# ScalarE's queue taken step by step, between engines that go two steps at a time, in a two-layer transformer kernel on one core

## The chip, the cores and the metric

The kernel runs on one core of a Trainium2 chip, as one launch. The metric is the device time in microseconds (us) of that launch; lower is better. TensorE (PE in the profile, its weight loads PEld), VectorE (DVE), ScalarE (ACT), GpSimd (POOL) and SyncE (SP, which here only issues DMAs) each run a queue of their own, written out by the kernel, and meet only at semaphores.

## The reference

Two layers over x of 32 batches x 256 tokens x 128 channels. Both have 16 heads of 8 channels and a mixture of 16 experts, of which each token takes two. Layer 0 has biases and a position term in its scores; layer 1 has an expert shared by all tokens in addition. Cut to what matters:

```python
h = _layernorm(x, axis=-1) * (1 + ca) + sa
x = x + ga * _L0_attn_ref(h, ...)      # scores = q k^T / sqrt(8) + slope * distance; softmax; probs v; Wo
h = _layernorm(x, axis=-1) * (1 + cb) + sb
x = x + gb * _L0_ffn_ref(h, ...)       # top 2 of 16 experts, gated, weighted sum
...                                    # modulation of layer 1
h = _layernorm(x, axis=-1) * (1 + ca) + sa
x = x + ga * _L1_attn_ref(h, ...)
h = _layernorm(x, axis=-1) * (1 + cb) + sb
x = x + gb * _L1_ffn_ref(h, ...)       # top 2 of 16 experts, and a shared expert
```

## The kernel before

**Units and steps.** A unit is one batch in one layer (64 units). Every engine walks over the same steps; a unit takes 16 of them until the next one follows, and each piece of a unit's work is tied to a step counted from the unit's start. Several units are therefore under way at once, at different stages. Steps run from -44 to beyond 1008.

**Scores and exponentials.** In each step TensorE makes, for one head of one unit, the scores with queries down (`ps_s`, L1230), of which VectorE takes the row maxima (`mx`, L1641), and, for one head of an earlier unit, the transposed scores with the maximum already subtracted (`ps_st`, L1236), of which ScalarE takes the exponential (`prob`, L877, 128x512). There are two banks of each. So the scores of step s wait until the maxima and the exponential of step s-2 are done (L1219 and L1224).

**Jobs.** All other matrix work of a step is in `jobs(step)`. It uses two PSUM banks, one for even and one for odd steps. By step modulo 16 (the constant `JOBS`):

- 0, 4, 8, 12: probabilities times values (`av`, L1099), copied out by ScalarE (`take_o`, L813) in the same step
- 1 and 11: the shared expert's first layer (L1195; layer 1 only), with a tanh on ScalarE (L866)
- 2 and 15: transposes of the attention result (L1107), read by VectorE
- 5: transposes of the normalised rows and of the context, each copied out by ScalarE (L805, L935)
- 6: transposes of the maxima and of the second normalised rows (L1157), each copied by ScalarE (L775, L943)
- 7: ranks of tokens among the experts, and the shared expert's second layer (L1203; layer 1 only), read by VectorE
- 9: projections of q and k (L1121), copied by ScalarE (L821/822 or L824/825)
- 10: output projection and router, read by VectorE; ScalarE makes the first bf16 part of q and k (L911), which needs nothing of this step
- 13: nothing on TensorE, a second bf16 part on ScalarE (L915)
- 14: transposes of the maxima and the values, each copied by ScalarE (L775, L927)
- 15 on ScalarE also: the normalisation (`xn`, L784)

**Experts.** Work on the experts comes in quads of four blocks with its own steps (transpose L1050, gate and up L1068, transpose L1080, down L1087), each followed by an activation on ScalarE (L834, L842 or L846, L853, L860). From about the sixteenth unit on three quads fall on every 32 steps, in even and odd steps, and in a job they come ahead of the unit's own work.

**Order of the queues.** TensorE's loop is by pairs: scores(s), scores(s+1), jobs(s), jobs(s+1). VectorE's is by pairs: maxima(s), maxima(s+1), rest(s), rest(s+1). ScalarE's is by pairs as well, with its exponentials in the place of the maxima; its `rest` holds all that is not an exponential. POOL's and SP's loops go by single steps. `free_bank` makes a job wait for the readers of the bank of two steps earlier. An engine's instructions go in the order of its queue, and a wait holds back all that is behind it.

Of the kernel before, what the change touches and what calls it, by code (L numbers as in the profile page):

```python
# [56 lines left out]
FIRST = -44  # L57
SETUP = -14
# [46 lines left out]
def at(step, after):  # L105

    n, k = divmod(step - after, H)
    return Unit(n) if k == 0 and 0 <= n < UNITS else None


def head_at(step, after):

    n, k = divmod(step - after, H)
    return (Unit(n), k) if 0 <= n < UNITS else (None, None)
# [20 lines left out]
STEPS = max(COMBINE) + 8  # L135
# [7 lines left out]
def quad_at(step, stage):  # L143

    for quick, after in enumerate(STAGE[stage]):
        q = Quad(QUAD[step - after]) if step - after in QUAD else None
        if q and q.quick == quick:
            return q
# [18 lines left out]
def build(nc, io, out):  # L167
    with ExitStack() as ctx:
# [215 lines left out]
        CLEAR = 6  # L384
# [366 lines left out]
        def _(sc):  # L751
# [6 lines left out]
            def setup():  # L758

                sc.wait_ge(rest_loaded, 16 * REST_LOADS)  # L760
                sc.activation(c_th[1][:], c_t[1][:], ACT.Tanh, scale=0.5).then_inc(c_tanh, 1)

            def clear_slots(i, part):

                if i == 0 and part == 0:
                    sc.wait_ge(dve_const, 6)
                n = NB // CLEAR
                sc.dma_start(slot_dram[i].rearrange("(j p) d -> p j d", p=P)[:, part * n:(part + 1) * n, :],
                             sh_out[:, 0:1, :].broadcast_to([P, n, D])).then_inc(slots_clear[i], 16)
# [39 lines left out]
            def take_o(u, g):  # L809
                sc.wait_ge(av_mm, u.count(4, g + 1))  # L810
                if g == 0 and u.has(2):
                    sc.wait_ge(ot_mm, u.count(2, -2))
                sc.activation(o_sb[u.par][:, g, :], ps_job[BANK[f"av{g}"]][:, 0:S], ACT.Copy).then_inc(o_ok, 1)  # L813
# [13 lines left out]
            def take_blocks(q):  # L827

                sc.wait_ge(blk_mm, q.no + 1)
                if q.no:  # L830
                    sc.wait_ge(gu_mm, q.before + 1)
                if q.tail and q.lane and q.nth == 0:
                    sc.wait_ge(av_mm, 4 * UNITS)
                sc.activation(h_blk_t[q.lane], ps_lane[q.bank][:], ACT.Copy).then_inc(blk_t_ok, 1)  # L834

            def tanh_gate(q):

                if q.no:
                    sc.wait_ge(*act_done(Quad(q.before)))
                if q.layer == 0:  # L840
                    sc.wait_ge(clip_ok, q.no * 2 + 1)
                    sc.activation(th_sb[0], g_sb[:].rearrange("p j f -> p (j f)"), ACT.Tanh, scale=0.5 * ALPHA).then_inc(th_ok, 1)  # L842
                else:
                    sc.wait_ge(gu_mm, q.no + 1)
                    gate = ps_lane[q.bank][:].rearrange("p (j g f) -> p j g f", j=QB, g=2)[:, :, 0, :]
                    sc.activation(th_sb[q.lane].rearrange("p (j f) -> p j f", j=QB), gate, ACT.Tanh, scale=0.5).then_inc(th_ok, 1)  # L846
# [8 lines left out]
            def take_y(q):  # L855

                sc.wait_ge(down_mm, q.no + 1)
                if q.no:
                    sc.wait_ge(*y_freed(q))
                sc.activation(y_sb[q.lane], ps_lane[q.bank][:], ACT.Copy).then_inc(y_ok, 1)  # L860
# [4 lines left out]
                    sc.wait_ge(sh_act_ok, u.count1(FC, c))  # L865
                sc.activation(sh_th[:], ps_job[BANK[f"sh{c}"]][:, 0:S], ACT.Tanh, scale=0.5).then_inc(sh_th_ok, 1)  # L866

            def exponentials(step):

                u, k = head_at(step, ST_AT)  # L870
                if u:
                    sc.wait_ge(st_mm, u.count(16, k + 1))
                    if k >= 8:
                        sc.wait_ge(av_mm, u.count(4, (k - 8) // 4 + 1))
                    elif u.has(1):
                        sc.wait_ge(av_mm, u.count(4, (k + 8) // 4 - 3))
                    sc.activation(prob[:, (k ^ 1) % 8, :], ps_st[k % 2][:], ACT.Exp).then_inc(exp_done, 1)  # L877

            def rest(step):

                for g in range(H // 4):
                    u = at(step, AT[f"av{g}"])
                    if u:
                        take_o(u, g)
                q = quad_at(step, "blocks")
                if q:
                    take_blocks(q)
                q = quad_at(step, "tanh")
                if q:
                    tanh_gate(q)  # L890
                q = quad_at(step, "act_t")
                if q:
                    take_act(q)
                q = quad_at(step, "down")
                if q:
                    take_y(q)
                u = at(step, -33)
                if u:
                    norm_apply(u)
                u = at(step, AT["h_t"])  # L900
                if u:
                    take_h(u)
                u = at(step, AT["qk"])
                if u:
                    take_qk(u)
                u = at(step, -22)
                if u:
                    sc.wait_ge(qk_ok, u.count(2, 2))
                    if u.has(1):
                        sc.wait_ge(parts_stored, u.count(96, 0))  # L910
                    sc.activation(qk_part[:, 0, :], qk_f[:], ACT.Copy).then_inc(qk_hi, 1)  # L911
                u = at(step, -19)
                if u:
                    sc.wait_ge(qk_r, u.count(1, 1))
                    sc.activation(qk_part[:, 1, :], qk_rest[:], ACT.Copy).then_inc(qk_mid, 1)  # L915
                for half in range(2):
                    u = at(step, AT[f"max_t{half}"])
                    if u:
                        take_max_t(u, half)
                u = at(step, AT["v"])  # L920
                if u:
                    sc.wait_ge(mxt0_v_mm, u.no + 1)
                    if u.has(2):
                        sc.wait_ge(av_mm, u.count(4, -4))
                    if u.no < 2:
                        sc.wait_ge(dve_const, 5)
                    sc.activation(v_ext[u.par][:, :, :, 0:DH],  # L927
                                  ps_job[BANK["v"]][:, S:2 * S].rearrange("p (t h d) -> p t h d", t=TT, h=H),
                                  ACT.Copy).then_inc(v_ok, 1)
                u = at(step, AT["ctx_t"])  # L930
                if u:
                    sc.wait_ge(h_ctx_mm, ctx_turn(u))
                    if u.has(1):
                        sc.wait_ge(wo_rt_mm, u.no)
                    sc.activation(ctx_t[:], ps_job[BANK["ctx_t"]][:, S:2 * S], ACT.Copy).then_inc(ctx_ok, 1)  # L935
                u = at(step, AT["h2_t"])
                if u:
                    sc.wait_ge(mxt1_h2_mm, h2_turn(u))
                    if u.has(1):
                        sc.wait_ge(wo_rt_mm, router_turn(u) - 1)  # L940
                    if u.no > B:
                        sc.wait_ge(sh_mm, u.count1(FC, 0))
                    sc.activation(h2_t[:], ps_job[BANK["h2_t"]][:, S:2 * S], ACT.Copy).then_inc(h2_ok, 1)  # L943
                for c in range(FC):
                    u = at(step, AT[f"sh{c}"])
                    if u and u.layer == 1:
                        tanh_shared(u, c)
                u = at(step, 77)
                if u:
                    sc.wait_ge(dz_ok, u.no + 1)  # L950
                    if u.layer == 1:
                        sc.wait_ge(z_ok, u.count1(1, 1))
                    if u.has(1):
                        sc.wait_ge(w_ok, u.count(2, 0))
                    if u.no > B:
                        sc.wait_ge(sg_ok, u.count1(1, 0))
                    n = 1 + u.layer
                    sc.activation(dz_th[:, 0:n, :], dz[:, 0:n, :], ACT.Tanh, scale=0.5).then_inc(top_tanh, 1)
                u = done_at(step, -2)
                if u:  # L960
                    first_rows(u)

            for step in range(FIRST, STEPS, 2):
                if step == SETUP:
                    setup()
                for s in (step, step + 1):
                    if s in range(40, 40 + 10 * 3 * CLEAR, 10):
                        clear_slots(*divmod((s - 40) // 10, CLEAR))
                exponentials(step)
                exponentials(step + 1)  # L970
                rest(step)
                rest(step + 1)


        @block.tensor
# [796 lines left out]
```

## Time and profile before

| | us |
|---|---|
| median of three runs | 1706.36 |
| lowest and highest of them | 1699.0, 1709.52 |
| the profiled execution | 1704.48 |
| its span, from first to last instruction | 1702.7 |

Busy shares of the span: TensorE 84%, VectorE 77%, ScalarE 68%, GpSimd 60%. Matmuls are pipelined and their ends are modelled, so TensorE's share is not a measure of its peak. The mean granted clock of TensorE was 0.948. The exponentials run from 75.9 us to 1528.4 us; behind that comes a tail of expert work. A row of the time-ordered view gives start and duration in us, then engine, line, operation, output and input, and in brackets the idle time in front of it and what ended it. Neighbouring equal instructions are merged into one row with their number (x2 for the two exponentials of a pair).

### The profile page before, as it was taken

The numbers are of one execution on the slowest core, as the hardware profiler recorded it, in microseconds if no ns is written. First come the engines' busy times: TensorE is split into PE (matmuls) and PEld (weight loads), VectorE is DVE, ScalarE is ACT, GpSimd is POOL, SyncE is SP. The second block draws the span as 40 slices with busy tenths as digits, with TensorE's granted clock in tenths as the row PEclk, the third lists the DMA queues.
The fourth block names the chain that finished last, engine by engine and source line by source line (L and its number), as shares of the span: only waits on it lengthen the run. The fifth ranks groups of instructions, "written<-read, shape, count | busy, mean of one in ns | idle before, by whom it ended". The sixth has DMA issues, their size and how long they took to land.

```text
span 1702.7 us, 44918 instructions
## 1 busy us (share of the span) xinstructions
PE 1425.2 (84%) x13909; PEld 920.9 (54%) x13909; DVE 1317.6 (77%) x3968; ACT 1163.5 (68%) x2708; POOL 1015.0 (60%) x1440
## 2 busy tenths in 40 slices
PE   2788887899899889988999989998999979886642
PEld 1244444465565556655666656665666646655542
DVE  5679898888888898889888898888888857643522
ACT  1488886788677777777777767777778757662422
POOL 1223336733675778577866778576756783577573
PEclk9999999999999999999999999999999989997966
DMA  6766666445555655566455656566556655344443
GB/s 202 174 149 158 154 153 147 127 118 124 137 144 129 141 126 148 139 143 141 122 146 139 133 125 153 132 142 137 136 142 157 145 127 126 102 118 128 138 129 86
DMA packets 392007, 234.70 MB, mean 138 GB/s; under 512 B 29007, under 2 KB 380561, under 8 KB 391267
## 3 DMA queue, kind: packets, MB, share of 16 engines
q1 hardware_dynamic: 356675, 188.82, 46.1%
q0 software_dynamic: 16384, 33.59, 7.4%
q10 hardware_dynamic: 18720, 9.44, 2.0%
q8 instruction: 121, 1.98, 0.5%
q14 instruction: 107, 0.88, 0.2%
HBM read 123.49 MB, written 108.17 MB: 136 GB/s over the span
## 4 chain that ended last, share of the span: by engine, by line
PE 36%; DVE 22%; POOL 22%; issue 13%; DMA 4%; ACT 1%; SPq 1%; POOLq 0%; DVEq 0%; ACTq 0%
DVE mx L1641 10%; POOL slot_dram L672 8%; PE ps_job L1099 7%; PE ps_s L1230 5%; POOL y_in L693 5%; PE ps_q L1068 4%; PE ps_q L1087 2%; PE ps_st L1236 2%; PE ps_q L1050 2%; PE ps_job L1120 2%; PE ps_q L1080 2%; POOL ln_rs L638 1%; PE ps_job L1195 1%; POOL qk_part L720 1%; PE ps_job L1203 1%
## 5 line engine op out<-in xcount | busy, mean ns | idle before, releaser
L1641 DVE TENSOR_REDUCE mx<-ps_s 128x2 f32<-128x512 f32 x1024 | 655.0, 681 | 107.8 <-PE ps_s L1230 105.9
L877 ACT ACTIVATE prob<-ps_st 128x512 f32<-128x512 f32 x1024 | 559.0, 595 | 80.7 <-PE ps_st L1236 80.1
L1230 PE MATMUL ps_s<-k_stk,q_stk 51*128 51x256 bf16 x2048 | 357.6, 282 | 89.9 <-DVE mx L1641 60.0
L1236 PE MATMUL ps_st<-q_stk,k_stk 53*128 53x256 bf16 x2048 | 350.9, 280 | 4.7 <-ACT prob L877 4.5
L1099 PE MATMUL ps_job<-prob,v_ext 128*32 128x256 f32 x4096 | 286.0, 398 | 24.8 <-issue 12.2
L672 POOL DMA_INDIRECT slot_dram<-h_row,slot x256 | 256.2, 1001 | 70.9 <-issue 64.2
L1230 PEld LDWEIGHTS ps_s<-k_stk,q_stk 51*128 51x128 bf16 x2048 | 142.5, 96 | 265.3 <-DVE mx L1641 163.4
L693 POOL DMA_INDIRECT y_in<-y_dram,slot x224 | 222.5, 993 | 84.8 <-issue 49.5
L1099 PEld LDWEIGHTS ps_job<-prob,v_ext 128*32 128x32 f32 x4096 | 115.9, 111 | 130.7 <-issue 31.3
L813 ACT ACTIVATE o_sb<-ps_job 128x256 f32<-128x256 f32 x256 | 96.8, 378 | 107.1 <-PE ps_job L1099 98.0
L716 POOL TENSOR_TENSOR qk_rest<-qk_f,qk_part 128x512 f32<-128x512 f32 x64 | 74.4, 1163 | 137.8 <-ACT qk_part L911 137.5
L1236 PEld LDWEIGHTS ps_st<-q_stk,k_stk 53*128 53x128 bf16 x2048 | 139.2, 96 | 16.5 <-ACT prob L877 6.3
L636 POOL TENSOR_SCALAR ln_ve<-ln_mv 128x2 f32<-128x2 f32 x128 | 28.8, 225 | 189.0 <-DVE ln_mv L1413 183.3
L1068 PE MATMUL ps_q<-wgu,h_blk_t 128*128 x704 | 116.3, 297 | 0.0
L1068 PEld LDWEIGHTS ps_q<-wgu,h_blk_t 128*128 128x128 f32 x704 | 98.6, 194 | 9.4 <-issue 7.7
L1087 PE MATMUL ps_q<-wd,act_t 128*128 x704 | 99.8, 285 | 3.1 <-ACT act_t L853 3.1
L720 POOL TENSOR_TENSOR qk_part<-qk_rest,qk_part 128x512 bf16<-128x512 f32 x64 | 74.3, 1160 | 41.7 <-ACT qk_part L915 41.1
L638 POOL TENSOR_TENSOR ln_rs<-ln_ve,neg_half 128x2 f32<-128x2 f32 x128 | 91.9, 718 | 10.7
L1087 PEld LDWEIGHTS ps_q<-wd,act_t 128*128 128x128 f32 x704 | 86.6, 194 | 19.7 <-issue 19.7
L1050 PE MATMUL ps_q<-ident,h_blk 128*128 128x128 f32 x376 | 65.8, 302 | 35.2 <-DMA h_blk<-slot_dram 30.3
L1107 PE MATMUL ps_job<-ident,o_sb 128*128 128x128 f32 x512 | 80.8, 282 | 1.2 <-DVE sh_act L1599 1.2
L711 POOL TENSOR_TENSOR act<-th_sb,u_sb 128x256 f32<-128x256 f32 x48 | 35.3, 734 | 68.3 <-DVE th_sb L1583 68.2
(211 smaller groups left out, 2885.8 us busy)
## 6 DMA issues: line engine op xcount, KB each, us to landing
part_dram<-qk_part SPq DMA_DIRECT2D x128, 192.0 KB
q_stk<-part_dram SPq DMA_DIRECT2D x128, 192.0 KB
k_stk<-part_dram SPq DMA_DIRECT2D x128, 192.0 KB
h_blk<-slot_dram SPq DMA_DIRECT2D x94, 256.0 KB, 3.2
y_dram<-y_sb SPq DMA_DIRECT2D x88, 256.0 KB, 2.4
part_dram<-qk_part SPq DMA_DIRECT2D x128, 128.0 KB
mod_in<-row_dram SPq DMA_DIRECT2D x64, 192.0 KB
slot_dram<-sh_out ACTq DMA_DIRECT2D x18, 512.0 KB, 4.6
```

The costliest lines, as they stand in the source:

```text
L638: pool.tensor_tensor(ln_rs[i][:], ln_ve[i][:], neg_half[:], ALU.pow).then_inc(ln_rstd[i], 1)
L672: pool.indirect_dma_start(slot_dram[u.group % 3], bass.IndirectOffsetOnAxis(ap=slot[u.group][:, i:i + 1], axis=0), h2_row[u.no % len(h2_ro ...
L693: pool.indirect_dma_start(y_rows[y_buf(u)[0]][:, j // 2, j % 2, :], None, y_dram[u.group % 3], bass.IndirectOffsetOnAxis(ap=slot[u.group][ ...
L813: sc.activation(o_sb[u.par][:, g, :], ps_job[BANK[f"av{g}"]][:, 0:S], ACT.Copy).then_inc(o_ok, 1)
L877: sc.activation(prob[:, (k ^ 1) % 8, :], ps_st[k % 2][:], ACT.Exp).then_inc(exp_done, 1)
L1050: mm = pe.transpose(ps_lane[q.bank][:, j * P:(j + 1) * P], h_blk[q.blk][:, j * D:(j + 1) * D], ident[:])
L1068: mm = pe.matmul(b[:, j * P:(j + 1) * P], h_blk_t[q.lane][:, j * P:(j + 1) * P], wgu[q.layer][:, w], start=q.layer == 1, stop=True)
L1087: mm = pe.matmul(ps_lane[q.bank][:, j * P:(j + 1) * P], act_t[q.lane][:, j * P:(j + 1) * P], wd[q.layer][:, bass.ds(expert[q.bank][j], P)] ...
L1099: mm = pe.matmul(columns(f"av{g}")[32 * i:32 * i + 32, 0:S], v_ext[u.par][:, kt, h, :], prob[:, h % 8, kt * S:(kt + 1) * S], start=kt == 0 ...
L1230: mm = pe.matmul(ps_s[j % 2][:, t * S:(t + 1) * S], q_stk[us.tri][r0:r0 + R_BIAS, hp, t * P:(t + 1) * P], k_stk[us.tri][r0:r0 + R_BIAS, hp ...
L1236: mm = pe.matmul(ps_st[k % 2][:, t * S:(t + 1) * S], k_stk[ut.tri][r1:r1 + R_MAX, hp, t * P:(t + 1) * P], q_stk[ut.tri][r1:r1 + R_MAX, hp, ...
L1641: dve.tensor_reduce(mx[:, hp // 4, :, 4 * par + hp % 4], ps_s[j % 2][:].rearrange("p (t s) -> p t s", s=S), AX_X, ALU.max).then_inc(max_do ...
```

## The change

ScalarE's loop becomes one over single steps: exponential of s, rest of s, exponential of s+1, rest of s+1. No instruction is added or removed, no semaphore value changes, and the loops of the other engines stay. What changes place, once per pair, is the exponential of the odd step s+1: it goes behind the rest of the even step s, with every wait in that rest. (The issue of a DMA that clears slots, which was ahead of a pair's exponentials, is now ahead of its own step's.)

```diff
-            def exponentials(step):
-
+            for step in range(FIRST, STEPS):
+                if step == SETUP:
+                    setup()
+                if step in range(40, 40 + 10 * 3 * CLEAR, 10):
+                    clear_slots(*divmod((step - 40) // 10, CLEAR))
                 u, k = head_at(step, ST_AT)
                 if u:
                     sc.wait_ge(st_mm, u.count(16, k + 1))
@@
                     sc.activation(prob[:, (k ^ 1) % 8, :], ps_st[k % 2][:], ACT.Exp).then_inc(exp_done, 1)
-
-            def rest(step):
-
                 for g in range(H // 4):
                     u = at(step, AT[f"av{g}"])
                     if u:
@@
-
-            for step in range(FIRST, STEPS, 2):
-                if step == SETUP:
-                    setup()
-                for s in (step, step + 1):
-                    if s in range(40, 40 + 10 * 3 * CLEAR, 10):
-                        clear_slots(*divmod((s - 40) // 10, CLEAR))
-                exponentials(step)
-                exponentials(step + 1)
-                rest(step)
-                rest(step + 1)
```

## Rows read from the trace of the kernel before

**Rows 1.** Stages of 50 us: busy us (instructions) by engine, clock, DMA share, GB/s
```profile
150.00:200.00 50.00, 43.13 (x493) 23.69 (x486) 45.03 (x141) 40.10 (x96) 15.82 (x33) 1.00 0.69 156
...
500.00:550.00 50.00, 46.67 (x486) 30.50 (x485) 41.59 (x123) 39.37 (x91) 26.17 (x41) 0.97 0.54 134
```

**Rows 2.** The same stages, exponentials (L877) alone: busy us (count), clock, DMA share
```profile
150.00:200.00 50.00, 25.04 (x47) 1.00 0.69 156
...
500.00:550.00 50.00, 19.78 (x36) 0.97 0.54 134
```

**Rows 3.** Waits of the whole span: us in total, times, longest
```profile
PEld ps_s L1230 <- DVE mx L1641: 163.4, 315, 4.0
...
DVE th_sb L1583 <- ACT th_sb L846: 33.6, 15, 3.8
...
PE ps_s L1230 <- ACT prob L877: 17.1, 33, 3.8
```

**Rows 4.** ScalarE in order of time, one unit without experts
```profile
161.17 1.08 ACT L877 ACTIVATE prob<-ps_st 128x512 f32<-128x512 f32 x2
162.12 0.65 ACT L911 ACTIVATE qk_part<-qk_f 128x512 bf16<-128x512 f32 x1
...
164.37 0.39 ACT L813 ACTIVATE o_sb<-ps_job 128x256 f32<-128x256 f32 x1 [0.63 <-PE ps_job L1099]
...
164.65 0.62 ACT L915 ACTIVATE qk_part<-qk_rest 128x512 bf16<-128x512 f32 x1
...
166.22 0.36 ACT L775 ACTIVATE mx_t<-ps_job 16x256 bf16<-16x256 bf16 x1
...
166.75 0.86 ACT L784 ACTIVATE xn<-x,ln_shift,ln_rs 128x128 f32<-128x128 f32 x2
```

**Rows 5.** TensorE in order of time, the same unit
```profile
160.34 0.28 PE L1230 MATMUL ps_s<-k_stk,q_stk 51*128 51x256 bf16 x1
...
162.40 0.27 PE L1230 MATMUL ps_s<-k_stk,q_stk 51*128 51x256 bf16 x1
...
163.25 1.07 PE L1099 MATMUL ps_job<-prob,v_ext 128*32 128x256 f32 x16 [0.45 <-issue]
164.25 0.28 PE L1230 MATMUL ps_s<-k_stk,q_stk 51*128 51x256 bf16 x1
...
164.48 0.27 PE L1230 MATMUL ps_s<-k_stk,q_stk 51*128 51x256 bf16 x1
...
165.57 0.60 PE L1107 MATMUL ps_job<-ident,o_sb 128*128 128x128 f32 x4
166.10 0.28 PE L1230 MATMUL ps_s<-k_stk,q_stk 51*128 51x256 bf16 x1
...
170.28 0.28 PE L1230 MATMUL ps_s<-k_stk,q_stk 51*128 51x256 bf16 x1 [0.58 <-DVE mx L1641]
...
177.52 0.28 PE L1230 MATMUL ps_s<-k_stk,q_stk 51*128 51x256 bf16 x1
```

**Rows 6.** GpSimd in order of time, one row of the same unit
```profile
162.85 1.16 POOL L716 TENSOR_TENSOR qk_rest<-qk_f,qk_part 128x512 f32<-128x512 f32 x1 [4.64 <-ACT qk_part L911]
```

**Rows 7.** ScalarE: first and last of 31 rows, a unit with experts, layer 0
```profile
502.81 1.08 ACT L877 ACTIVATE prob<-ps_st 128x512 f32<-128x512 f32 x2 [0.82 <-PE ps_st L1236]
...
522.92 1.10 ACT L877 ACTIVATE prob<-ps_st 128x512 f32<-128x512 f32 x2
```

**Rows 8.** ScalarE: first and last of 33 rows, a unit of layer 1
```profile
1060.41 1.08 ACT L877 ACTIVATE prob<-ps_st 128x512 f32<-128x512 f32 x2
...
1083.24 1.08 ACT L877 ACTIVATE prob<-ps_st 128x512 f32<-128x512 f32 x2
```

**Rows 9.** TensorE in order of time: two jobs of odd steps, a clock dip
```profile
805.21 1.93 PE L1099 MATMUL ps_job<-prob,v_ext 128*32 128x256 f32 x16 [0.59 <-issue]
...
1064.40 1.14 PE L1203 MATMUL ps_job<-wsd,sh_act 128*128 128x128 f32 x8
...
1079.57 1.13 PE L1195 MATMUL ps_job<-h_t,wsgu 128*128 128x256 f32 x4
```

## The prediction

> **What bounds the kernel now.** I read the stages of 50 us first, then the waits, then the order of time engine by engine. In a stage without experts (150 to 200 us) VectorE is busy 45.0 of 50 us, TensorE 43.1, ScalarE 40.1; from 500 to 550 us, with experts, TensorE 46.7, VectorE 41.6, ScalarE 39.4 [rows 1]. No engine is full. The exponentials give the pace: 47 in 50 us, or 1.06 us a step, in the first, 36 or 1.39 us in the second [rows 2]. The waits show a ring of TensorE and VectorE, alternately late: TensorE's score loads waited 163.4 us for maxima, and its score matmuls only 17.1 us, 33 times, for an exponential [rows 3]. So ScalarE is now hardly ever late at the scores. It has slack, and the question is how much of it the new order takes.
>
> The order of time shows why. The pair's exponentials follow the scores at once, and they fill the very time in which TensorE does the even step's job: the exponentials of steps 12 and 13 lie ahead of 163.6, and the values' matmul of step 12 runs from 163.25 to 164.25; ScalarE then sat idle 0.63 us and copied its result at 164.37 [rows 4, 5]. With the new order only one exponential fills that gap; the other has to come after the copy.
>
> **The change, part by part.** No instruction is added, and the work per pair is the same, so there is no cost in busy time. A pair starts with two steps of scores on TensorE; then come J(s) and J(s+1), the job times. The exponential of s+1 must be done before the scores of s+3, the second step of the next pair.
> - Before, it starts about half a microsecond behind that of s. Two take 1.08 us, and the next activation starts 0.95 us after the first [rows 4], so each occupies 0.48.
> - After, it starts 0.05 us (rounded from the gap seen at the value's copy) behind the end of J(s), plus R, the issue time of the even step's activations that wait for J(s).
> - From the start of an exponential to the scores that it releases are 0.75 us: the second of the pair at 161.17 starts at 161.65, and the scores of step 13 at 162.40 [rows 4, 5].
> - Left to itself TensorE would start the scores of s+3 at the end of J(s) plus J(s+1) plus 0.23 (164.25 to 164.48) [rows 5].
>
> The lateness is therefore 0.05 + R + 0.75 - 0.23 - J(s+1) = R + 0.57 - J(s+1). For the eight pairs of a unit without experts:
> - 12: R 0.28 (164.37 to 164.65), J(13) nothing: 0.85. The same at 0 in layer 0, where step 1 is empty.
> - 14: two copies, R 0.53 (166.22 to 166.75), J(15) 0.53 (165.57 to 166.10): 0.57 [rows 4, 5].
> - 4: R 0.28, J(5) four transposes like J(15), some 0.55: 0.30.
> - 6: R as at 14; J(7) a few 16-column matmuls, an estimate of 0.25: 0.85.
> - 10: no wait for the job, but the q and k part goes ahead of the second exponential, 0.52 us from 162.12 on [rows 4]; that exponential was already the last thing awaited at 162.40, so 0.52.
> - 8: J(9), two projections, is longer than R + 0.57: nothing. 2: nothing on ScalarE in its rest: nothing.
>
> The sum is 3.9 us in a unit of 17.18 us (160.34 to 177.52) [rows 5]. It isn't all paid, since TensorE also waits for maxima: at 170.28 it sat 0.58 us for them [rows 5]. I carried the new order by hand through this unit, each start the latest of its own queue, its operand and its bank, with VectorE's queue in the same manner. The stalls at steps 15, 1 and 3 add up to about 1.65; VectorE's maxima take back 0.9 to 1.0 at steps 4 and 5; steps 7 and 9 add 0.3 and 0.4. Step 13 adds another 0.25, because the job behind it waits for VectorE until 163.25 anyway. The end is later by 1.3 to 1.55: say 1.45.
>
> With experts, a quad in an odd job lengthens J(s+1) and hides the late exponential; one in an even job adds half a microsecond to R. The same walk through the layer-0 unit that starts at 502.81 (20.11 us) [rows 7] ends 1.0 to 1.1 later. Nothing is lost at step 15 (a quad in step 13); the rest comes at steps 1, 7, 9, 11 and 13. In layer 1 the shared expert puts about 1.1 us each into steps 7, 11 and 1 [rows 9], which clears the lateness at 0 and 6; but the copies and quads of even steps, up to three activations ahead of an exponential, put it back: the walk through the 22.83 us from 1060.41 [rows 8] ends 1.4 later.
>
> Sum: the first 14.5 units run before the experts start, 14.5 x 1.45 = 21; 17.5 units of layer 0 with experts x 1.1 = 19; 32 of layer 1 x 1.4 = 45; together 85 us. Nine units end a group, where VectorE plans for about 3 us and everything else waits for it; I take those as absorbing all of theirs, 9 x 1.3 = 12. That leaves 73. Before the first exponential and after the last nothing changes, since a rest follows a rest as before. 1704.5 + 73 = 1777.5 for the profiled execution, which lies 1.9 under the median; I forecast 1778.
>
> **Does a queue let a ready activation pass?** The whole sum rests on the exponential being held by the copies in front. The trace bears it out: the q and k part at 164.65 needed only GpSimd's result of 164.01 (162.85 + 1.16), yet ScalarE idled until 164.37 for the copy ahead of it [rows 4, 6]. The Trainium skill, "TensorE: Matmul & The Clock Gate", section "Architectural detail", says that ScalarE and VectorE queues are strictly first in, first out; by that rule the sum stands, and had it not held, the lateness would be nought and the time that of before.
>
> **The rivals.**
> - *Hidden*: VectorE is the real pacer and swallows the lateness wherever TensorE would have waited for maxima. For it: 163.4 us of such waits [rows 3], twice my sum. Against: they come in 315 small pieces, and a late set of scores delays the next maxima too, which the walk includes. In full it gives 1706, within 1%; at half, 1704.5 + 37 = 1742.
> - *Faster*: copies of an even step no longer stand behind the second exponential and come up to 0.48 us earlier. It decides where J(s) ends before that exponential does and someone waits for the copy. VectorE's wait for an expert's tanh, 33.6 us in 15 waits [rows 3], is the largest such place; all gone, with the lateness hidden, gives about 1670. Against it: at 164.37 ScalarE had been idle, so the exponentials weren't what held the copy [rows 4]; and in my walks the copies come no earlier at most places.
> - *Clock*: more gaps on TensorE, more stretches at a lower granted clock. In one such stretch behind a long wait the sixteen value matmuls took 1.93 us instead of 1.07 [rows 5, 9]. Some 2 us for each further dip, one for every three units, is 20 x 2 = 40: 1704.5 + 73 + 40 = 1818. Against: the new gaps are below 1 us each, and stage 150 to 200 has full clock with gaps of that size [rows 1].
>
> **How the numbers follow.** Lateness as summed 0.58; hidden for the greater part 0.14 (half of that within 1%); clock or a ring that costs more than my sum 0.21; faster 0.07. The forecast is that of the likeliest, 1778. The low end is halfway hidden, 1742, taken to 1738; the high end is the clock's 1818. Beyond them lie the fully hidden case, faster, and a part of the worst: two in ten. About 1% is what a measurement of this kernel can tell from no change. Faster by more than 1%: 0.06; within 1%: 0.09; slower by more: 0.85.
>
> **What would show it.** TensorE's waits for L877 rise from 17.1 us to several times that, and ScalarE's idle time in front of copies (L813, L775) rises, with busy time of all engines unchanged. A unit without experts takes some 18.6 us instead of 17.18, and its stage holds 43 or 44 exponentials in 50 us, not 47. The stretch behind the last exponential keeps its length. In order of time, a row L877 x1 stands behind each L813. It would be wrong if TensorE's waits for L877 grow while those for L1641 shrink by as much (hidden), or if the granted clock falls clearly below 0.948 (clock).

## The result, and the profile after

The changed kernel took 1768.57 us (median of four runs, 1760.37 to 1770.07) beside 1702.68 for the kernel before (four runs): a ratio of 1.0357, 95% interval 1.0322 to 1.0393 (the quotient of the two medians, 1.039, lies within it). It is slower by some 61 to 66 us. The profiled executions are 1769.74 us (span 1768.0) and 1704.48 (span 1702.7), 65.3 us apart. The mean granted clock of TensorE is 0.948 in both.

The head of the page after; the columns are busy time, share of the span and count:

```profile
span 1768.0 us, 44918 instructions
## 1 busy us (share of the span) xinstructions
PE 1447.1 (82%) x13909; PEld 911.2 (52%) x13909; DVE 1328.6 (75%) x3968; ACT 1151.2 (65%) x2708; POOL 1015.2 (57%) x1440
```

Every engine has as many instructions as before, and its busy time moved by 22 us at most. The time went into waiting. The waits after, us in total, times, longest:

```profile
ACT o_sb L813 <- PE ps_job L1088: 233.5, 253, 4.0
PEld ps_s L1219 <- issue: 204.3, 491, 3.5
PEld ps_s L1219 <- DVE mx L1630: 160.5, 279, 2.8
...
PE ps_s L1219 <- ACT prob L880: 115.6, 247, 3.3
...
ACT prob L880 <- PE ps_st L1225: 50.8, 74, 2.3
```

The third and the fourth row answer to [rows 3]: TensorE's score matmuls waited 17.1 us, 33 times, for an exponential, and now 115.6 us, 247 times. The weight loads' wait for maxima stayed where it was, 163.4 and 160.5 us; the score matmuls' own wait for maxima, which [rows 3] doesn't show, fell from 60.0 to 43.0 us. The second row, in which no releaser is named, was 87.5 us before; in the unit below it names loads of the very scores that come late (at 180.43 a load 1.01 us, at 180.46 its matmul 0.76 us for the exponential), so it is for a good part the same lateness again. ScalarE stood in front of the values' copy 253 of 256 times. (Line numbers of the changed kernel differ: L877 is L880, L1230 is L1219, L1641 is L1630, L1099 is L1088.)

The stages of [rows 1] and [rows 2], after: busy us and count of each engine, clock, DMA share and GB/s, then the exponentials alone:

```profile
150.00:200.00 50.00, 40.24 (x456) 21.66 (x450) 41.92 (x132) 38.30 (x89) 16.11 (x32) 1.00 0.63 153
...
500.00:550.00 50.00, 44.91 (x475) 27.92 (x473) 41.08 (x121) 37.21 (x87) 33.45 (x49) 1.00 0.50 136
```

```profile
150.00:200.00 50.00, 24.53 (x43) 1.00 0.63 153
```

43 exponentials in the first stage, where there were 47; both TensorE and VectorE are less busy in it. A unit without experts, on TensorE in order of time, answers to [rows 5]. These are all the matmul rows of it with a wait for an exponential or a maximum:

```profile
172.96 0.27 PE L1219 MATMUL ps_s<-k_stk,q_stk 51*128 51x256 bf16 x1 [0.52 <-ACT prob L880]
...
175.44 0.27 PE L1219 MATMUL ps_s<-k_stk,q_stk 51*128 51x256 bf16 x1 [0.75 <-DVE mx L1630]
...
177.98 0.27 PE L1219 MATMUL ps_s<-k_stk,q_stk 51*128 51x256 bf16 x1 [0.53 <-ACT prob L880]
...
180.46 0.27 PE L1219 MATMUL ps_s<-k_stk,q_stk 51*128 51x256 bf16 x1 [0.76 <-ACT prob L880]
...
184.27 0.27 PE L1219 MATMUL ps_s<-k_stk,q_stk 51*128 51x256 bf16 x1 [0.17 <-ACT prob L880]
...
186.53 0.27 PE L1219 MATMUL ps_s<-k_stk,q_stk 51*128 51x256 bf16 x1 [0.66 <-ACT prob L880]
```

They are the scores of steps 13, 15, 1, 3, 7 and 9, always the second step of a pair. That the second row names VectorE is put right by the order of time: VectorE had already finished the maxima of step 13 at 174.37 (173.10 + 1.27), while the exponential ran until 175.29, as ScalarE's queue shows, in the place of the pair of [rows 4]:

```profile
174.42 0.38 ACT L813 ACTIVATE o_sb<-ps_job 128x256 f32<-128x256 f32 x1 [1.12 <-PE ps_job L1088]
...
174.70 0.59 ACT L880 ACTIVATE prob<-ps_st 128x512 f32<-128x512 f32 x1
175.18 0.63 ACT L915 ACTIVATE qk_part<-qk_rest 128x512 bf16<-128x512 f32 x1
```

ScalarE idled 1.12 us with the exponential of step 13 behind the copy, then the copy, then the exponential, and 0.74 us after its start (174.70 to 175.44) TensorE went on.

To see how the loss is spread I took the start of the first values' copy (L813) of each unit. The distance from one to the next is the unit's time. Sums in us:

| stretch | before | after | difference |
|---|---|---|---|
| first 14 units, nearly all without experts | 249.9 | 272.6 | 22.7 |
| the next 17, layer 0 with experts | 385.1 | 398.6 | 13.5 |
| the next 24, layer 1 | 571.1 | 591.7 | 20.6 |
| the rest of layer 1, to the last copy | 246.1 | 251.0 | 4.9 |
| ahead of the first copy, and behind the last | 250.5 | 254.1 | 3.6 |

### The profile page after: what moved, and what is told of

The parts are those of the page before. It is cut to its first block, busy times and chain, and to the rows that moved or that the text cites. A ratio compares the mean times of both kernels' runs of the same rounds, so it can differ in the third digit from the quotient of the medians.

```text
span 1768.0 us, 44918 instructions
## 1 busy us (share of the span) xinstructions
PE 1447.1 (82%) x13909; PEld 911.2 (52%) x13909; DVE 1328.6 (75%) x3968; ACT 1151.2 (65%) x2708; POOL 1015.2 (57%) x1440
## 4 chain that ended last, share of the span: by engine, by line
PE 37%; POOL 18%; issue 15%; DVE 15%; ACT 11%; DMA 2%; ACTq 0%; SPq 0%; POOLq 0%; DVEq 0%
PE ps_job L1088 10%; DVE mx L1630 7%; PE ps_s L1219 6%; POOL slot_dram L672 6%; ACT prob L880 6%; POOL y_in L693 4%; PE ps_q L1057 4%; PE ps_q L1076 2%; PE ps_job L1184 2%; PE ps_q L1039 1%; PE ps_job L1192 1%; PE ps_q L1069 1%; PE ps_st L1225 1%; PE ps_job L1139 1%; DVE y_two L1608 1%
## 5 line engine op out<-in xcount | busy, mean ns | idle before, releaser
L1630 DVE TENSOR_REDUCE mx<-ps_s 128x2 f32<-128x512 f32 x1024 | 664.5, 684 | 136.1 <-PE ps_s L1219 132.8
L880 ACT ACTIVATE prob<-ps_st 128x512 f32<-128x512 f32 x1024 | 601.7, 595 | 52.6 <-PE ps_st L1225 50.8
L1219 PE MATMUL ps_s<-k_stk,q_stk 51*128 51x256 bf16 x2048 | 380.3, 280 | 164.2 <-ACT prob L880 115.6
L1225 PE MATMUL ps_st<-q_stk,k_stk 53*128 53x256 bf16 x2048 | 379.8, 280 | 6.6 <-ACT prob L880 6.6
L1219 PEld LDWEIGHTS ps_s<-k_stk,q_stk 51*128 51x128 bf16 x2048 | 131.9, 95 | 378.6 <-issue 204.3
L1088 PE MATMUL ps_job<-prob,v_ext 128*32 128x256 f32 x4096 | 287.7, 400 | 6.7 <-issue 4.7
L813 ACT ACTIVATE o_sb<-ps_job 128x256 f32<-128x256 f32 x256 | 98.1, 383 | 234.6 <-PE ps_job L1088 233.5
L1088 PEld LDWEIGHTS ps_job<-prob,v_ext 128*32 128x32 f32 x4096 | 111.2, 112 | 111.1 <-issue 51.8
L1225 PEld LDWEIGHTS ps_st<-q_stk,k_stk 53*128 53x128 bf16 x2048 | 124.7, 95 | 15.0 <-ACT prob L880 8.8
L775 ACT ACTIVATE mx_t<-ps_job 16x256 bf16<-16x256 bf16 x128 | 47.3, 370 | 53.2 <-PE ps_job L1146 35.6
```

The costliest lines, as they stand in the source:

```text
L1088: mm = pe.matmul(columns(f"av{g}")[32 * i:32 * i + 32, 0:S], v_ext[u.par][:, kt, h, :], prob[:, h % 8, kt * S:(kt + 1) * S], start=kt == 0 ...
L1219: mm = pe.matmul(ps_s[j % 2][:, t * S:(t + 1) * S], q_stk[us.tri][r0:r0 + R_BIAS, hp, t * P:(t + 1) * P], k_stk[us.tri][r0:r0 + R_BIAS, hp ...
L1225: mm = pe.matmul(ps_st[k % 2][:, t * S:(t + 1) * S], k_stk[ut.tri][r1:r1 + R_MAX, hp, t * P:(t + 1) * P], q_stk[ut.tri][r1:r1 + R_MAX, hp, ...
L1630: dve.tensor_reduce(mx[:, hp // 4, :, 4 * par + hp % 4], ps_s[j % 2][:].rearrange("p (t s) -> p t s", s=S), AX_X, ALU.max).then_inc(max_do ...
```

## The experiments

Two things have to be known for all of them. First, they ran on four chips, each beside the kernel before. On one of these the kernel before took 1705 us, on the other three 1806 to 1810 us (the faster and the slower kind below), so only ratios are compared between chips, and with care. Second, a unit without experts repeats to a few hundredths of a microsecond, on both kinds of chip: most take 17.18 to 17.22 us before and 18.53 to 18.60 after. The median of the third to the twelfth unit is given below as "period"; it is 17.19 and 17.21 for the kernel before on the two kinds of chip, 18.54 and 18.55 for the changed one.

Most kernels change only the condition in ScalarE's loop, which was written so that the new order can be had pair by pair:

```diff
                 exponentials(step)
-                exponentials(step + 1)
-                rest(step)
+                if <condition>:
+                    rest(step)
+                    exponentials(step + 1)
+                else:
+                    exponentials(step + 1)
+                    rest(step)
                 rest(step + 1)
```

### Is the loss where the formula puts it?

Condition `step % H in (0, 4, 6, 10, 12, 14)`:

> ScalarE takes the new order only in the pairs whose even step is 0, 4, 6, 10, 12 or 14 modulo 16 (those for which the prediction's formula gives a lateness), the old one in pairs 2 and 8. Theory (the exponential behind the even step's copies comes late for the scores of s+3): all or nearly all of the loss, ratio to the kernel before 1.032 to 1.040. Rival (every interleaved pair costs the same, whatever stands in its rest, by lost back-to-back issue): six eighths, ratio about 1.027.

Condition `step % H in (2, 8)`:

> The new order only in pairs 2 and 8, the complement of the former. Theory: 0 to 6 us slower, ratio 1.000 to 1.004; what there is comes from quads that fall on these even steps. Rival (every pair the same): two eighths, ratio about 1.009.

And the changed kernel unchanged, on a chip of the slower kind:

> The changed kernel, unchanged, beside the single parts. Theory: the part with the six pairs that come late by the formula was the whole of it, so the ratio here is within 0.006 of that part's on a chip of the same kind (1.053 on the slower one, about 1.036 on the first). Rival (parts add up over all pairs): clearly above it.

Measured: six pairs 1.0528 (1.0466 to 1.0591), two pairs 1.0120 (1.0057 to 1.0183), all eight 1.0675 (1.0626 to 1.0724). The change costs nearly twice as much on this kind of chip as on the first. The six pairs are four fifths of it, not all: the whole lies 0.015 above them, where I had expected 0.006 at most. By total time the expectation for the two "free" pairs fell too, and equal shares fit better (six eighths and two eighths of 6.75% are 5.1% and 1.7%, both inside the intervals). The periods say why both are half right: 18.54 with the six pairs, the whole of the loss of a unit without experts, and 17.21 with the two, none of it. So where no expert work is about, the formula picks the right pairs; what pairs 2 and 8 cost is in the units with experts, where a quad's activation comes into their rest. The waits bear this out: TensorE's score matmuls waited 47.7 us for exponentials in that run and 15.6 in the kernel before on a chip of that kind. I had allowed 6 us for it; it is about 22 of 1806, with an interval from 10 to 33.

### Do the lateness terms add up?

Conditions `step % H in (0, 12)`, `(4, 6)` and `(10, 14)`:

> The new order only in pairs 0 and 12, where a copy of the attention values stands ahead of the exponential and the odd step has no job in layer 0. Theory: 1.7 of the 3.9 us of raw lateness, so about 0.4 of the loss, 25 to 32 us, ratio 1.015 to 1.019. Rival (every pair the same): ratio about 1.009. Third: if the lateness of other pairs is mostly carried by these two, more than 40 us, ratio over 1.024.

> The new order only in pairs 4 and 6. Formula of the prediction: 1.15 of 3.9 us raw. Additive: about 0.3 of the loss; ratio 1.015 to 1.02 on a chip where the whole is 1.0675. After the run with pairs 0 and 12, which cost 1.2 us over the first fourteen units where the formula gave 1.7 raw each, a single stall seems to be absorbed by VectorE's waits unless another follows: then pairs 4 and 6, whose jobs bring two copies each, cost more than 0 and 12 did, but less than their share, ratio 1.01 to 1.02, and parts add up to less than the whole.

> The new order only in pairs 10 and 14. Formula: 1.09 of 3.9 us raw, near a VectorE-bound job each. Additive: ratio 1.015 to 1.02. If single stalls are absorbed: below 1.01. If the loss of the six pairs (1.053) is neither in 0 and 12 (1.014) nor in 4 and 6, it has to show here, over 1.02.

| new order in pairs | ratio (95% interval) | period | formula, raw |
|---|---|---|---|
| 0, 12 | 1.0142 (1.0087 to 1.0198), slower kind of chip | 17.41 (+0.20) | 1.70 |
| 4, 6 | 1.0147 (1.0109 to 1.0185), faster kind | 17.88 (+0.69), most units 17.85 | 1.15 |
| 10, 14 | 1.0033 (1.0012 to 1.0055), faster kind | 16.82 (-0.37) | 1.09 |
| 2, 8 | 1.0120 (1.0057 to 1.0183), slower kind | 17.21 (0.00) | 0 |
| all | 1.0357 and 1.0675 | 18.54 (+1.35) | 3.9 |

They don't add up in the period: 0.20 + 0.69 - 0.37 is 0.52, against 1.35. With pairs 0 and 12 alone both stalls are there on TensorE and in nearly full size, yet the unit grows by 0.2 us only (TensorE in order of time, in that run):

```profile
165.34 0.27 PE L1234 MATMUL ps_s<-k_stk,q_stk 51*128 51x256 bf16 x1 [0.75 <-ACT prob L877]
...
169.65 0.27 PE L1234 MATMUL ps_s<-k_stk,q_stk 51*128 51x256 bf16 x1 [0.59 <-ACT prob L877]
```

What takes these stalls back is a wait that was there anyway. The kernel before has these in the same stretch, at the scores of steps 3, 5 and 9, besides the 0.58 us for maxima at step 4 [rows 5]:

```profile
168.23 0.27 PE L1230 MATMUL ps_s<-k_stk,q_stk 51*128 51x256 bf16 x1 [0.22 <-ACT prob L877]
...
170.88 0.28 PE L1230 MATMUL ps_s<-k_stk,q_stk 51*128 51x256 bf16 x1 [0.20 <-DVE mx L1641]
...
174.53 0.27 PE L1230 MATMUL ps_s<-k_stk,q_stk 51*128 51x256 bf16 x1 [0.26 <-ACT prob L877]
```

With pairs 0 and 12 the scores come late at steps 15 and 3, ahead of the two waits for maxima at steps 4 and 5, and neither of the two (0.78 us) is among the waits of that unit any more. With pairs 4 and 6 the scores come late at steps 7 and 9, behind them. Both waits are still there, and 0.69 us is paid of the 0.83 that those two steps wait (in that run):

```profile
172.91 0.28 PE L1234 MATMUL ps_s<-k_stk,q_stk 51*128 51x256 bf16 x1 [0.57 <-DVE mx L1645]
...
173.50 0.28 PE L1234 MATMUL ps_s<-k_stk,q_stk 51*128 51x256 bf16 x1 [0.21 <-DVE mx L1645]
...
176.15 0.27 PE L1234 MATMUL ps_s<-k_stk,q_stk 51*128 51x256 bf16 x1 [0.17 <-ACT prob L877]
...
178.41 0.27 PE L1234 MATMUL ps_s<-k_stk,q_stk 51*128 51x256 bf16 x1 [0.66 <-ACT prob L877]
```

So it isn't the number of stalls that decides, but whether a wait for the other engine follows. With all pairs in the new order the waits at steps 4 and 5 are gone as well, but they can be used up only once. Total time says less here than the period: the losses of the parts, taken on different kinds of chip, add up to 4.4%, between the 3.6% and the 6.8% of the whole.

Pairs 10 and 14 even shorten the period, which neither theory had. TensorE does wait there (0.52 and 0.53 us for exponentials), but the waits of 0.58 and 0.20 us for maxima at steps 4 and 5 are down to 0.17 and 0.20, and that of 0.45 us in front of the values' matmul of step 12 [rows 5] is gone: VectorE is earlier. One row of it changed its length (in that run):

```profile
166.22 0.21 DVE L1487 TENSOR_TENSOR hot<-idx,iota_e 128x64 bf16<-128x64 uint32 x1
```

In the kernel before the same operation started at 164.25 and took 0.68 us, ending 0.09 after GpSimd's addition (164.12 to 164.84):

```profile
164.12 0.72 POOL L705 TENSOR_TENSOR x<-x,att_tmp 128x256 f32<-128x256 f32 x1
```

The 0.47 us is more than the gain. The later it starts in GpSimd's addition, the shorter it is, and the end stays where it was: two units further on, in the kernel before, the addition ran from 198.48 to 199.21, and the operation ended at 199.28.

```profile
198.93 0.35 DVE L1483 TENSOR_TENSOR hot<-idx,iota_e 128x64 bf16<-128x64 uint32 x1
```

In 18 of the 64 units of the kernel before it starts while that addition still has 0.15 us or more to run; it takes 0.27 to 0.73 us there and ends 0.08 to 0.09 us behind the addition in all 18. So it is held until GpSimd is done; what holds it the traces don't show, and no run takes the addition away. With the new order in pairs 10 and 14 it starts only 0.11 us before the addition ends. The changed kernel does the same, so this gain is part of its 1.35 us already:

```profile
174.29 0.22 DVE L1472 TENSOR_TENSOR hot<-idx,iota_e 128x64 bf16<-128x64 uint32 x1
```

I did try the gain itself, with the condition `step < 258 and step % H in (10, 14)`:

> The new order only in pairs 10 and 14 and only up to step 257, before the experts start. In the run with pairs 10 and 14 everywhere a unit without experts took 16.82 us instead of 17.19, while units with experts grew. If that gain holds by itself and nothing later takes it back: 10 to 12 units x 0.37 = 4 us faster, ratio 0.996 to 0.999, unit period 16.82 again. Rival (the gain is taken back by the first experts, or the period depends on how the queues happen to stand): ratio 1.000 or above.

The period was 16.84 again, but the whole ratio 1.0019 (0.9991 to 1.0047, slower kind of chip). 3 us in 1807 can't be told from nothing. No version here beats the kernel before.

### Does the loss add up over the stages?

Condition `step < 258`:

> The new order only up to step 257, before the experts' quads start; 14.5 units. Theory: 14.5 x 1.45 = 21 us, 17 to 24, ratio 1.010 to 1.014. Rival (the loss comes mostly from the experts' activations, which stand in the way of the exponentials): under 10 us, ratio below 1.006.

Measured 1.0177 (1.0129 to 1.0226) beside 1.0675 for the whole on the same chip. That is above the 1.010 to 1.014 that I had expected (the interval just reaches into it), and far above the rival's 1.006. The period is 18.55, the whole loss of such a unit. The first 14 units took 26.5 us longer than in the profile of the kernel before on that chip, of 34 in all; 8.2 of this is in the very first, which I had counted like the others. The changed kernel loses 26.6 in them. So a stage pays its own loss, and what is late there is not won back later.

### Is it the mismatch with TensorE, or single steps as such?

TensorE, VectorE and ScalarE all by single steps:

```diff
 scores(step)
-scores(step + 1)
 jobs(step)
+scores(step + 1)
 jobs(step + 1)
```

(and the same in VectorE's loop, on top of the changed ScalarE loop)

> TensorE, VectorE and ScalarE all go by single steps. Theory (it is the mismatch: TensorE asks for two exponentials before the job's copies, ScalarE gives one): TensorE's waits for exponentials fall back under 40 us, as the exponential of s+1 has the whole of job s+1 and of job s+2 as cover; the time is nearer to before than to after, if VectorE's single order costs nothing of its own: ratio 0.99 to 1.02. Rival (single steps on ScalarE are bad in themselves): ratio 1.03 or more, with the waits for exponentials still above 80 us.

ScalarE by single steps, exponentials a step ahead:

```diff
-            for step in range(FIRST, STEPS, 2):
+            for step in range(FIRST, STEPS + 2):
...
-                exponentials(step)
-                exponentials(step + 1)
-                rest(step)
-                rest(step + 1)
+                exponentials(step)
+                rest(step - 1)
```

> ScalarE by single steps, but with the exponentials one step ahead: exponential of s, rest of s-1, exponential of s+1, rest of s. No exponential has a copy of its own pair's even job in front of it. Theory (the cause is the wait for job s ahead of the exponential of s+1): the loss goes, ratio 0.990 to 1.015, TensorE's waits for exponentials under 40 us. Rival (interleaving single exponentials and copies costs by itself, by lost back-to-back issue): ratio near that of the change, 1.035 or more.

All single: 1.0115 (1.0052 to 1.0177), against 1.0675 on a chip of the same kind; the period is 17.02. TensorE's score matmuls waited 12.2 us for exponentials:

```profile
PE ps_s L1234 <- ACT prob L877: 12.2, 27, 1.1
```

The same ScalarE queue as in the changed kernel costs five sixths less once its neighbours go in the same rhythm. What is left isn't in the units without experts, which are 0.2 us shorter than before. (TensorE and VectorE were changed together; which of the two mattered more wasn't tried, but the wait for exponentials is TensorE's.)

A step ahead: 1.0190 (1.0149 to 1.0231), period 17.64. Half of the loss of 1.0357 is gone, and not all; of the 1.35 us of a unit 0.45 is left. The cause that I wanted to take away is away; the wait turned round instead:

```profile
ACT prob L877 <- PE ps_st L1233: 294.1, 328, 6.6
...
PE ps_s L1227 <- ACT prob L877: 32.3, 54, 2.8
```

ScalarE waited 294.1 us for scores (80.1 before), with the copies of the step before behind it. An example is the exponential of step 10, behind which the q and k copies stood in the queue, though their projections had ended by 162.70:

```profile
163.10 0.60 ACT L877 ACTIVATE prob<-ps_st 128x512 f32<-128x512 f32 x1 [1.01 <-PE ps_st L1233]
163.59 0.47 ACT L821 ACTIVATE qk_f<-ps_job,bq_s 128x256 f32<-128x256 f32 x1
```

So my expectation of 0.990 to 1.015 was too good: I had looked only at what is ahead of the exponential, and not at what it stands ahead of.

### The mirror image

VectorE alone by single steps, ScalarE in pairs as before:

> ScalarE in pairs as before; VectorE alone by single steps: its maxima of s+1 go behind its rest of s. The mirror image of the change. Theory (whoever reads the second score bank late holds up the scores of s+3): VectorE is busier and its rest longer, so the loss is at least that of the change: ratio 1.035 to 1.09, and TensorE's waits for maxima rise from about 220 us by 60 us or more. Rival (what counted was the exponential, since maxima are awaited anyway): ratio below 1.015.

1.0645 (1.0597 to 1.0693), on the same chip as the changed kernel's 1.0675. TensorE's score matmuls and their weight loads waited for maxima 174.7 and 285.5 us; in the kernel before on this chip it was 52.5 and 145.3:

```profile
PEld ps_s L1230 <- DVE mx L1641: 285.5, 326, 4.6
...
PE ps_s L1230 <- DVE mx L1641: 174.7, 187, 4.3
```

Either reader of the two score banks does it. That VectorE is busier didn't make it worse by these two ratios. In the units without experts it did: their median is 19.6 us, against 18.55 for the changed kernel. The granted clock was lower as well, 0.89 to 0.90 in these runs against 0.914 to 0.923; how much of the time that is can't be told from these runs.

### The slower chips

> The kernel before, unchanged, for a profile on the chip of the other runs. Expected: the same queues and waits as in the first profile; if the chip is as slow as that of the last four runs (1805.6 us against 1702.7), the profile shows which waits are longer there.

It took 1805.89 us. Its period is 17.21, that of the first chip; up to the eleventh unit the two differ by little (but for the first, 15.0 and 16.6 us). Units with experts differ: a median of 24.7 us against 22.1 for those of layer 0, while some of them (20.6 us) are the same on both. New in the waits are rows like these, whose releaser the profile can't name on the core:

```profile
ACT o_sb L813 <- remote: 49.0, 15, 7.4
...
DVE mx L1641 <- remote: 29.2, 13, 4.4
```

In one such place VectorE (4.82 us) and ScalarE (3.46 us) stood still and resumed within 0.1 us of each other, though the last of TensorE's transposed scores that ScalarE needed shows as started at 454.65:

```profile
454.65 0.27 PE L1236 MATMUL ps_st<-q_stk,k_stk 53*128 53x256 bf16 x1
...
458.31 0.42 DVE L1574 TENSOR_SCALAR g_sb<-ps_q 128x256 f32<-128x256 f32 x1 [4.82 <-remote]
458.39 1.08 ACT L877 ACTIVATE prob<-ps_st 128x512 f32<-128x512 f32 x2 [3.46 <-remote]
```

What holds them isn't shown. No profile taken on the faster kind of chip has such a row. The granted clock is lower too: 0.917 to 0.937 in the runs of the kernel before on the slower chips, 0.944 to 0.956 on the faster one. Nor is it shown why the change costs twice as much there. The unnamed waits don't grow with it (49.0 and 29.2 us before, 48.0 and 28.9 after); the clock falls a little, from 0.920 to 0.933 on that chip to 0.914 to 0.923. What is shown is that the difference lies in units with experts (median of layer 0 26.3 after, 24.7 before) and not in the period.

## Why the prediction was right

**The mechanism.** It said that the exponential of s+1, held by the even step's copies, would come late for the scores of s+3. The rows of the result show that at each pair that it named. Its signs came true: the granted clock stayed, the busy times moved by 22 us at most, and the stretch behind the last exponential kept its length to about 2 us (173.8 and 171.7). The formula's terms beside the waits of one unit: step 13, 0.52 and 0.52; step 15, 0.85 and 0.75; step 1, 0.57 and 0.53; step 3, 0.85 and 0.76; step 7, 0.30 and 0.17; step 9, 0.85 and 0.66; none at 5 and 11, as it said. The sum is 3.94 against 3.39. The 0.75 us from an exponential's start to the scores was 0.74.

**What is paid of it.** 1.45 us for a unit without experts, by hand; measured 1.35 in the steady stretch, a period of 18.54 against the 18.6 that it gave, 43 exponentials in the stage against its 43 or 44. Its split holds in the main. It put 1.65 us into steps 15, 1 and 3; they wait 2.04 us, 0.22 of which was there before. It took 0.9 to 1.0 back at steps 4 and 5; the two waits that vanish there are 0.78. It put 0.7 into steps 7 and 9; these wait 0.83, 0.26 of which was there before, and alone cost 0.69. It didn't foresee that VectorE's operation of step 10 would be 0.46 us shorter in the new order; without that, the 1.35 might well have been more, and the agreement to 0.1 us is in part luck.

**The sum.** 21 us for the units without experts; 22.7 for the first 14. That is close partly by luck: the first two cost 6.5 together, more than two steady units, and the last two nothing (0.07). For layer 0 with experts it gave 19 less four absorbing units at 1.3, some 14 us; 13.5 were lost (a median of 1.04 a unit, forecast 1.1). For layer 1 it gave 45 less five such units, 38.5 us; 25.5 were lost, and this is the mis-sized term. Two things went into it. The walked unit was a little dear: the 21 units of layer 1 that took 24.6 us or less before lost 1.15 us each, against 1.4 (4.65 of it in the last unit alone). And more units swallow their lateness than the five that end a group: eleven units of layer 1 took over 24.6 us before, and lost 2.0 together. (Over both layers it is 14 of the 49 units from the fifteenth on, with 1.2 us. That they wait for something else is what their length suggests; which wait it is isn't shown, and the limit of 24.6 us was chosen afterwards.) Ahead of the first copy and behind the last another 3.6 us were lost, where the sum has nothing. So 73 became 65.3, inside the range.

**The rivals.** *Hidden* is refuted for the whole (the weight loads' waits for maxima were 163.4 and 160.5 us, and the matmuls' own fell by 17.0 us, while the waits for exponentials grew by 98.5), but its mechanism is real for pairs 0 and 12, where all but 0.20 of 1.34 us vanish. *Clock* is refuted on that chip: 0.948 in both. *Faster* is refuted as a whole; copies did not come earlier, since ScalarE idled 233.5 us in front of them. A small gain exists in pairs 10 and 14, for another reason than the one given.

**First in, first out.** The prediction leaned on the Trainium skill, "TensorE: Matmul & The Clock Gate", section "Architectural detail", for ScalarE's strict order. The traces agree: 1.12 us idle at 174.42 with an exponential behind whose scores were ready, and 1.01 us at 163.10 in the run a step ahead, with copies behind whose job was done.

## What to carry to other kernels

Here a producer handed out work in batches of two and double-buffered by bank, and it didn't pay for a consumer to turn to something that waits for the producer's next phase before it had taken the whole batch; one queue with a finer grain than its neighbours cost more than three of them with the finer grain (1.0675 against 1.0115). Price such an order by pair: what stands ahead of the late item, against what the producer still does before it asks. Then look for waits of the producer that follow each stall, since they take it back, and only once, and count the units that wait for something else anyway.

## What the runs showed that I had not expected

- The same kernel takes 1703 to 1705 us on some chips and 1806 to 1810 on others, with a period of 17.19 to 17.21 us without experts on both kinds; a change that costs 3.6% on one kind costs 6.8% on the other. A ratio belongs to the chip it was taken on.
- Two stalls of 0.75 and 0.59 us ahead of a wait for maxima lengthened a unit by 0.20 us; two of 0.17 and 0.66 us behind it by 0.69; six of 3.39 us in sum by 1.35.
- A reordering that made TensorE wait 0.5 us for an exponential at two steps of a unit shortened the unit by 0.37 us, beside a VectorE operation that took 0.21 instead of 0.68 us. In 18 units of the kernel before this operation ended 0.08 to 0.09 us behind a GpSimd operation during which it had started, however late that was.
